# The order of the message sums on TensorE in a three-layer graph network kernel

## The chip, the cores and the metric

The kernel runs on one core of one Trainium2 chip. Time is device time in microseconds (us) of one execution; a comparison goes by the median of several runs. The profile is of one execution on the chip.

## What is computed

A graph network of three layers over 20,000 nodes with 512 features, and 5,000 edges sorted by their end node. Cut to what matters:

```
for Wl, bl, Wr, g, b in three layers:
    msg = h[src]
    agg = segment_sum(msg, dst) / max(count, 1)
    h   = residual + agg @ Wl.T + bl + h @ Wr.T
    h   = layer_norm(h, g, b)
    h   = prelu(h);  residual = h
out = layer_norm(x + h)
```

## The kernel before, in words

**Tiles and units.** Nodes are put into slots so that all nodes on which an edge ends lie in the first 40 tiles of 128 slots; the other tiles have no messages. Tiles are worked in pairs, called units. A layer has 20 *edge units* (two tiles with messages) and 59 *plain units*. The order of units is made by `order(lead)`: first `lead` plain units, then edge units with plain units between them. In the first two layers the lead is 20 units, and two plain units stand between an edge unit and the next. In the last layer the lead is 8 units, and of its 19 gaps between edge units 12 hold three plain units and 7 hold two. `Unit(no)` gives a unit's tiles, its layer and its buffers.

**TensorE** (`tensor_program`, the loop over T from L489 on) goes through the units; T is the unit in work, `ahead` is unit T+1. A step is:

- `turn(ahead)`: 8 transposes 128x128 of the next unit's rows (L402), into `ps_t`.
- If the next unit is an edge unit, `sum_messages(ahead, 0)` and `sum_messages(ahead, 1)`: 4 matmuls each (L414) that sum the gathered messages `msg[j]` by a 0/1-like matrix `same[j]` into `ps_s[j]`, one call for each tile j. Each waits for three things: the matrix (`e_same`, from VectorE), the gathered rows (`m_in[j]`, a DMA), and that the sums of the edge unit before were taken out of `ps_s[j]` (`e_carry`).
- `product_self(u, 0)`, `product_self(u, 1)`: the products of the unit in work with its own features, 12 matmuls of 512 columns for each tile (three for each of 4 chunks, since numbers are split into a high and a low part; L422, with `hT_hi`, `hT_lo`). They wait for `low` (the split, from VectorE) and `filled` (the bias rows, from ScalarE).
- For an edge unit in work, `product_mean(u, 0)` and `(u, 1)`: 12 such matmuls for each tile with the sums (L422, `sT_hi`, `sT_lo`).

All engines run their own written list in order, and meet by semaphores; TensorE passes its list strictly from top to bottom.

**GpSimd** (POOL) has, in step T: `root(T)` (L742; in the last layer also L746), then in the last layer `put_out` of unit T-5 (two indirect DMAs of output rows, L764), then in the first layer `gather_x`, then `gather_messages` of unit T+3 if that is an edge unit (two indirect DMAs, L731, one for each tile: `msg[0]`, then `msg[1]`). `gather_messages` waits until both sums of the edge unit before are done.

**SyncE** (SP) loads 512 KB of rows for a unit (`load_h`, L302), in the last layer also 512 KB for the residual (`load_residual`, L330), and for an edge unit 256 KB of row table (`load_rowtab`, L312), all in one list.

**VectorE and ScalarE** split the transposed rows (L535, L866), fill the bias (L575), take the squares of the products (L544), scale and shift (L877, L898), apply the prelu (L904), and for edge units make `same` (L915), carry the sums on (`carry`, L930) and split them (L584, L938).

The lines that order the work in a step of TensorE are:

Of the kernel before, what the change touches and what calls it, by code (L numbers as in the profile page):

```python
# [22 lines left out]
def reach(eng, sem, count):  # L23

    if count > 0:
        eng.wait_ge(sem, count)


def build_program(nc, x, wT, bl, g, b, a_prelu, ident_in, const_in, edge_cols_in, edge_last_in, edge_rows_in,
# [59 lines left out]
    with ExitStack() as ctx:  # L89
# [277 lines left out]
        def tensor_program(pe):  # L367
            def count_signs(i):

                pe.wait_ge(split_out, i + 1)  # L370
                begin, end = i == ET - SHARE, i == 2 * ET - SHARE - 1
                pe.matmul(signs_a, ones_short[:], tiles_above[i % HB], start=begin, stop=end)
                pe.matmul(signs_b, places_from[i % HB], tiles_above[i % HB], start=begin, stop=end).then_inc(counted, 1)
# [19 lines left out]
            def turn(u):  # L393
                if u.l == 0:
                    for j in range(u.n):
                        pe.wait_ge(x_in[u.r3][j], 16 * (u.no // 3 + 1))
                else:
                    pe.wait_ge(h_in[u.r3], 16 * (u.no // 3 + 1 - uses(u.r3, 3, UL)))
                reach(pe, low, u.no)
                for j in range(u.n):  # L400
                    for k in range(KC):
                        mm = pe.transpose(ps_t[:, j, k * P:(k + 1) * P], hin[u.r3][:, j, k * P:(k + 1) * P], ident[:])  # L402
                mm.then_inc(turned, 1)

            def sum_messages(u, j):
                if not u.edge:
                    return
                if u.eno == 0:
                    pe.wait_ge(table_done, 3)
                pe.wait_ge(e_same, 2 * u.eno + j + 1)  # L410
                pe.wait_ge(m_in[j], 16 * (u.eno + 1))
                reach(pe, e_carry, 2 * u.eno + j - 1)
                for k in range(KC):
                    mm = pe.matmul(ps_s[j][:, k * P:(k + 1) * P], msg[j][:, k * P:(k + 1) * P], same[j][:],  # L414
                                   start=True, stop=True)
                mm.then_inc(e_summed, 1)
# [9 lines left out]
            def product_self(u, j):  # L426
                if j >= u.n:
                    return
                if j == 0:
                    pe.wait_ge(low, u.no + 1)  # L430
                    if u.pos == 0:
                        pe.wait_ge(w_low, KC * (2 * u.l + 1))
                pe.wait_ge(filled, u.ahead + j + 1)
                mm = mm3(ps_z[u.r2][:, j, :], hT_hi[u.r2][:, j], hT_lo[u.r2][:, j], 2 * u.l, not u.edge)
                if not u.edge:
                    mm.then_inc(z_ready, 1)

            def product_mean(u, j):
                if not u.edge:
                    return  # L440
                if u.tiles[0] == 0 and j == 0:
                    pe.wait_ge(w_low, KC * (2 * u.l + 2))
                pe.wait_ge(e_low, 2 * u.eno + j + 1)
                mm3(ps_z[u.r2][:, j, :], sT_hi[j], sT_lo[j], 2 * u.l + 1, True).then_inc(z_ready, 1)

            def turn_table(parts):
                for j, (t0, t1) in enumerate(parts):
                    mm = pe.transpose(ps_s[0][0:t1 - t0, j * P:(j + 1) * P], table[:, t0:t1], ident[:])
                mm.then_inc(table_turned, 1)
# [31 lines left out]
            for T in range(UNITS):  # L481
                ahead, u = Unit(T + 1), Unit(T)
                if T == 0:
                    product_self(u, 0)

                    pe.wait_ge(row_step, 4)
                    pe.transpose(last_runs, run[:, P - 1:P], ident[0:ET, 0:ET]).then_inc(small, 1)
                if ahead.exists:
                    turn(ahead)  # L489
                if T == 0:  # L490
                    pe.wait_ge(row_step, 5)
                    pe.transpose(ahead_turned, runs_ahead[0:1, 0:ET], ident[0:1, 0:1]).then_inc(small, 1)
                for i in range(ET):
                    if T == COUNT_SLOT + 1 + i // COUNTS_A_SLOT:
                        if i == 0:
                            pe.wait_ge(table_done, 1)
                            pe.wait_ge(row_step, 6)
                        count_signs(ET - SHARE + i)
                if ahead.exists:
                    sum_messages(ahead, 0)  # L500
                if T > 0:
                    product_self(u, 0)
                if ahead.exists:
                    sum_messages(ahead, 1)
                product_self(u, 1)
                product_mean(u, 0)
                product_mean(u, 1)
                if T == TABLE_SLOT + 1:
                    pe.wait_ge(count_read, 2)
                    turn_table([(0, P), (P, NT)])  # L510
# [576 lines left out]
        with nc.Block() as block:  # L1087
            block.sync(sync_program)
            block.tensor(tensor_program)
            block.scalar(scalar_program)  # L1090
            block.gpsimd(gpsimd_program)
            block.vector(vector_program)
# [57 lines left out]
```

## Time and profile before

| | |
|---|---|
| median of 3 runs | 2011.26 us (2010.85 to 2011.39) |
| profiled execution, its own time | 2011.12 us |
| its span | 2009.3 us |
| TensorE matmul busy | 1974.9 us (98%) |
| VectorE busy | 1597.0 us (79%) |
| ScalarE busy | 1220.8 us (61%) |
| GpSimd busy | 924.1 us (46%) |
| matmuls of the sums (L414) | 960 records, 126.6 us busy |
| DMA, mean | 193 GB/s |

The profiled execution's own time is 1.8 us more than its span; what lies outside the span is taken as fixed. Times in the rows are counted from the start of the span. "Busy" of matmuls overlaps, as they are pipelined: what one costs is read from the distance between starts, not from its duration. One f32 matmul of L414 leaves two records.

The first layer lies at about 30 to 690 us, the second to about 1330 us, the last to 1980 us.

### The profile page before, as it was taken

What the parts mean: (1) busy time and instruction counts of PE and PEld (TensorE: products, weight loads), DVE (VectorE), ACT (ScalarE), POOL (GpSimd) and SP (SyncE); (2) the same over time, 40 slices, a digit from 0 to 9 for tenths busy, and PEclk for the clock granted to TensorE, in tenths of its full rate; (3) what the DMA queues carried; (4) which work ended last, traced back from release to release, by engine and by line L of the source; (5) the groups of instructions that cost most, each with busy time, mean ns of one, the idle gap of its engine ahead of it and who ended that gap; (6) DMA issues with size and microseconds to landing.
All of it is one profiled execution on the core that took longest, in us unless ns stands there. A gap on an engine that the chain in (4) does not pass through costs nothing. (4 is left out here: it accounts for less than half of the span.)

```text
span 2009.3 us, 30530 instructions
## 1 busy us (share of the span) xinstructions
PE 1974.9 (98%) x10207; PEld 1659.7 (83%) x10207; DVE 1597.0 (79%) x2598; ACT 1220.8 (61%) x2669; POOL 924.1 (46%) x887
## 2 busy tenths in 40 slices
PE   9999999999999999999999999999999999999994
PEld 7888888888888888888888888888888888888883
DVE  7778777777777677877777777769989998898985
ACT  6864545554444455544444444458878887787875
POOL 2666566556555411322333333215555455454555
PEclk9999999999999999999999999999999999999997
DMA  6667766766666555544444444456666666666652
GB/s 208 229 228 261 220 218 222 231 208 205 206 207 208 168 158 170 177 143 150 158 151 143 158 154 151 146 168 200 225 210 216 219 224 201 214 231 196 233 194 108
DMA packets 181075, 387.69 MB, mean 193 GB/s; under 512 B 20117, under 2 KB 20562, under 8 KB 180918
## 3 DMA queue, kind: packets, MB, share of 16 engines
q1 hardware_dynamic: 142358, 272.06, 40.6%
q0 software_dynamic: 38560, 113.67, 17.4%
q8 instruction: 82, 1.34, 0.3%
q14 instruction: 75, 0.61, 0.1%
HBM read 221.07 MB, written 164.79 MB: 192 GB/s over the span
## 5 line engine op out<-in xcount | busy, mean ns | idle before, releaser
L422 PE MATMUL ps_z<-w_hi,hT_hi 128*128 128x512 f32 x1884 | 763.0, 405 | 0.9 <-DVE hT_lo L866 0.6
L422 PE MATMUL ps_z<-w_hi,hT_lo 128*128 128x512 f32 x1884 | 738.6, 392 | 0.0
L422 PE MATMUL ps_z<-w_lo,hT_hi 128*128 128x512 f32 x1884 | 737.8, 392 | 0.0
L742 POOL TENSOR_TENSOR rstd<-veps,minus_half 128x2 f32<-128x2 f32 (+1 forms) x237 | 237.2, 1001 | 866.3 <-ACT veps L554 866.1
L866 DVE TENSOR_TENSOR hT_lo<-ps_t,hT_hi 128x1024 fp32r<-128x1024 f32 (+1 forms) x237 | 288.0, 1215 | 312.9 <-ACT hT_hi L535 309.5
L575 ACT COPY ps_z<-bias_rows 128x512 f32<-128x512 f32 x471 | 276.7, 588 | 344.6 <-DVE y L877 332.8
L544 ACT ACTIVATE junk<-ps_z 128x512 f32<-128x512 f32 x471 | 278.5, 592 | 307.1 <-PE ps_z L422 306.9
L422 PEld LDWEIGHTS ps_z<-w_hi,hT_lo 128*128 128x128 f32 x1884 | 353.5, 188 | 79.0
L422 PEld LDWEIGHTS ps_z<-w_hi,hT_hi 128*128 128x128 f32 x1884 | 354.5, 188 | 68.5 <-DVE hT_lo L866 1.0
L422 PEld LDWEIGHTS ps_z<-w_lo,hT_hi 128*128 128x128 f32 x1884 | 354.8, 188 | 67.0
L877 DVE SCALAR_TENSOR_TENSOR y<-ps_z,rstd,gain 128x512 f32<-128x512 f32 x471 | 330.1, 742 | 1.1 <-POOL rstd L742 1.0
L904 DVE SCALAR_TENSOR_TENSOR hout<-y,slope 128x1024 f32<-128x1024 f32 (+1 forms) x237 | 301.3, 1271 | 0.1
L898 DVE TENSOR_TENSOR y<-y,shift 128x1024 f32<-128x1024 f32 (+1 forms) x237 | 290.2, 1225 | 8.1
L402 PEld LDWEIGHTS ps_t<-ident,hin 128*128 128x128 f32 x1884 | 220.0, 140 | 31.8 <-issue 0.7
L402 PE MATMUL ps_t<-ident,hin 128*128 128x128 f32 x1884 | 244.4, 272 | 0.1
L535 ACT CAST hT_hi<-ps_t 128x1024 fp32r<-128x1024 f32 (+1 forms) x237 | 234.7, 990 | 6.3 <-PE ps_t L402 6.0
L764 POOL DMA_INDIRECT out<-o_sb,node_put x157 | 166.9, 1063 | 68.1 <-issue 50.7
L422 PE MATMUL ps_z<-w_hi,sT_lo 128*128 128x512 f32 x480 | 188.0, 392 | 0.0
L422 PE MATMUL ps_z<-w_hi,sT_hi 128*128 128x512 f32 x480 | 187.7, 391 | 0.0
L422 PE MATMUL ps_z<-w_lo,sT_hi 128*128 128x512 f32 x480 | 187.7, 391 | 0.0
L708 POOL DMA_INDIRECT hin<-in_x,node_get x157 | 157.2, 1001 | 63.4 <-issue 36.2
L611 ACT ACTIVATE o_sb<-o_sb,omove,rstd 128x512 f32<-128x512 f32 x157 | 119.6, 809 | 73.4 <-POOL omove L746 70.5
(147 smaller groups left out, 1927.6 us busy)
## 6 DMA issues: line engine op xcount, KB each, us to landing
h_scratch<-hout SPq DMA_DIRECT2D x156, 512.0 KB, 3.2
hin<-h_scratch SPq DMA_DIRECT2D x156, 512.0 KB, 4.3
x_by_slot<-hin SPq DMA_DIRECT2D x78, 512.0 KB, 3.2
o_sb<-x_by_slot SPq DMA_DIRECT2D x78, 512.0 KB, 4.6
rowtab<-edge_row_table SPq DMA_DIRECT2D x60, 256.0 KB, 4.7
stage<-in_WrT SPq DMA_DIRECT2D x3, 1024.0 KB, 8.8
stage<-in_WlT SPq DMA_DIRECT2D x3, 1024.0 KB, 7.5
hin<-in_x,node_get POOLq DMA_INDIRECT x157, 3.7
```

The source lines that it names most:

```text
L402: mm = pe.transpose(ps_t[:, j, k * P:(k + 1) * P], hin[u.r3][:, j, k * P:(k + 1) * P], ident[:])
L422: mm = pe.matmul(acc, a[:, k, :], ww[:, k, :], start=False, skip_group_check=True, stop=stop and k == KC - 1 and a is a_lo)
L535: nc.scalar.copy(hT_hi[u.r2][:, 0:u.n].rearrange("p j k n -> p (j k n)"), ps_t[:, 0:u.n, :].rearrange("p j d -> p (j d)")).then_inc(high, 1)
L544: nc.scalar.activation(junk[j][:], ps_z[u.r2][:, j, :], ACT.Square, accum_out=ssq[u.r2][:, j:j + 1]).then_inc(squared, 1)
L575: nc.scalar.copy(ps_z[u.r2][:, j, :], bias_rows[:, u.l, :]).then_inc(filled, 1)
L708: pool.indirect_dma_start(hin[u.r3][:, j, :], None, x, bass.IndirectOffsetOnAxis(node_get[:, t:t + 1], 0)).then_inc(x_in[u.r3][j], 16)
L742: nc.gpsimd.tensor_tensor(rstd[(T - 1) % 2][:, at], veps[(T - 1) % 2][:, at], minus_half[:, at], ALU.pow).then_inc(rstd_done, 1)
L764: pool.indirect_dma_start(out, bass.IndirectOffsetOnAxis(node_put[:, t:t + 1], 0), o_sb[u.ring][:, j, :], None, bounds_check=N - 1, oob_is ...
L866: nc.vector.tensor_tensor(hT_lo[u.r2][:, 0:u.n].rearrange("p j k n -> p (j k n)"), ps_t[:, 0:u.n, :].rearrange("p j d -> p (j d)"), hT_hi[ ...
L877: nc.vector.scalar_tensor_tensor(y[u.r2][:, j, :], ps_z[u.r2][:, j, :], rstd[u.r2][:, j:j + 1], gain[:, u.l, :], ALU.mult, ALU.mult).then_ ...
L898: nc.vector.tensor_tensor(y[u.r2][:, 0:u.n, :], y[u.r2][:, 0:u.n, :], moved, ALU.add).then_inc(shifted, 1)
L904: nc.vector.scalar_tensor_tensor(hout[u.r3][:, 0:u.n, :], y[u.r2][:, 0:u.n, :], slope[:, 0:1], y[u.r2][:, 0:u.n, :], ALU.mult, ALU.max).th ...
```

## The change

In a step whose next unit is an edge unit, TensorE now does the sums of both tiles one behind the other, and then the products of the unit in work. Before, the sum of tile 1 stood between the products of tile 0 and those of tile 1.

```diff
                 if ahead.exists:
                     sum_messages(ahead, 0)
+                    sum_messages(ahead, 1)
                 if T > 0:
                     product_self(u, 0)
-                if ahead.exists:
-                    sum_messages(ahead, 1)
                 product_self(u, 1)
                 product_mean(u, 0)
                 product_mean(u, 1)
```

No other engine's list changes. In TensorE's list this is the step ahead of the first edge unit, before (the rows of the twelve products that only repeat are left out):

```order
725 L414 MATMUL ps_s0<-same0,msg0 128x128 [waits m_in0,e_same,table_done]
726 L414 MATMUL ps_s0<-same0,msg0 128x128 x3
727 L422 MATMUL ps_z1<-w_hi0,hT_hi1 128x512 [waits filled,low]
...
738 L422 MATMUL ps_z1<-w_hi0,hT_lo1 128x512
739 L414 MATMUL ps_s1<-same1,msg1 128x128 [waits m_in1,e_same,table_done]
740 L414 MATMUL ps_s1<-same1,msg1 128x128 x3
741 L422 MATMUL ps_z1<-w_hi0,hT_hi1 128x512 [waits filled]
```

The sum of tile 1, with its wait for `m_in1`, stands behind the 12 products of tile 0. The same place in the changed kernel:

```order
725 L414 MATMUL ps_s0<-same0,msg0 128x128 [waits m_in0,e_same,table_done]
726 L414 MATMUL ps_s0<-same0,msg0 128x128 x3
727 L414 MATMUL ps_s1<-same1,msg1 128x128 [waits m_in1,e_same,table_done]
728 L414 MATMUL ps_s1<-same1,msg1 128x128 x3
729 L422 MATMUL ps_z1<-w_hi0,hT_hi1 128x512 [waits filled,low]
...
741 L422 MATMUL ps_z1<-w_hi0,hT_hi1 128x512 [waits filled]
```

The wait for `m_in1` now stands ahead of all 24 products of the step, and the number of instructions is the same. There are 60 such steps, 20 in each layer.

## Rows read from the trace of the kernel before

**Rows 1.** Last layer: stretch; PE, PEld, DVE, ACT, POOL busy; PEclk, DMA share, GB/s.

```profile
1400.00:1960.00 560.00, 560.00 (x2893) 474.66 (x2893) 510.78 (x928) 451.24 (x978) 300.66 (x306) 1.00 0.64 214
```

**Rows 2.** Timeline of PE (start, duration) around one edge step of the second layer.

```profile
1024.66 1.03 PE L402 MATMUL ps_t<-ident,hin 128*128 128x128 f32 x8
1025.53 1.06 PE L414 MATMUL ps_s<-same,msg 128*128 128x128 f32 x8
1026.35 0.48 PE L422 MATMUL ps_z<-w_hi,hT_hi 128*128 128x512 f32 x1
...
1032.79 1.03 PE L402 MATMUL ps_t<-ident,hin 128*128 128x128 f32 x8
1033.58 0.48 PE L422 MATMUL ps_z<-w_hi,hT_hi 128*128 128x512 f32 x1
...
1039.14 0.39 PE L422 MATMUL ps_z<-w_hi,sT_hi 128*128 128x512 f32 x1
```

**Rows 3.** Message gathers (L731) of the first layer, and its last sum's start on PE.

```profile
L731 POOL DMA_INDIRECT msg<-in_x,edge_cols x38: 952/1428/1950, 173.8 to 658.5; - x38
...
DMA to landing us min/median/max: 3.6/4.4/7.8
...
670.81 0.28 PE L414 MATMUL ps_s<-same,msg 128*128 128x128 f32 x1
```

**Rows 4.** The same for the second layer.

```profile
L731 POOL DMA_INDIRECT msg<-h_scratch,src_slot x38: 942/1018/1653, 824.9 to 1299.7; - x38
...
DMA to landing us min/median/max: 3.4/3.7/4.8
...
1314.61 0.28 PE L414 MATMUL ps_s<-same,msg 128*128 128x128 f32 x1
```

**Rows 5.** Last layer, first edge unit: gather of tile 1, sums on PE.

```profile
L731 POOL DMA_INDIRECT msg<-h_scratch,src_slot x1: 1910/1910/1910, 1377.8 to 1377.8; - x1
...
DMA to landing us min/median/max: 8.9/8.9/8.9
...
1382.57 1.06 PE L414 MATMUL ps_s<-same,msg 128*128 128x128 f32 x8
...
1386.82 1.13 PE L414 MATMUL ps_s<-same,msg 128*128 128x128 f32 x8
```

**Rows 6.** Last layer, third edge unit: gather of tile 1, first sum.

```profile
L731 POOL DMA_INDIRECT msg<-h_scratch,src_slot x1: 1907/1907/1907, 1435.9 to 1435.9; - x1
...
DMA to landing us min/median/max: 8.3/8.3/8.3
...
1442.18 0.28 PE L414 MATMUL ps_s<-same,msg 128*128 128x128 f32 x1
```

**Rows 7.** Last layer, 17th edge unit: gather of tile 1, first sum.

```profile
L731 POOL DMA_INDIRECT msg<-h_scratch,src_slot x1: 1911/1911/1911, 1860.9 to 1860.9; - x1
...
DMA to landing us min/median/max: 8.7/8.7/8.7
...
1867.22 1.06 PE L414 MATMUL ps_s<-same,msg 128*128 128x128 f32 x8
```

**Rows 8.** Timeline of SP at that place: loads issued.

```profile
1860.76 0.33 SPq L312 DMA_DIRECT2D rowtab<-edge_row_table  x1
1861.18 0.39 SPq L302 DMA_DIRECT2D hin<-h_scratch  x1
1861.66 0.42 SPq L330 DMA_DIRECT2D o_sb<-x_by_slot  x1
```

**Rows 9.** Busy time by stretch after PE's last matmul (columns of rows 1).

```profile
1980.30:1983.90 3.60, 0.00 (x0) 0.00 (x0) 3.50 (x7) 3.57 (x9) 2.71 (x5) 1.00 0.01 2
1984.00:1994.00 10.00, 0.00 (x0) 0.00 (x0) 5.10 (x12) 7.75 (x17) 7.80 (x11) 0.50 0.35 132
```

**Rows 10.** Timeline of PE at the start of the span.

```profile
2.22 2.07 PE L460 MATMUL ps_z<-nought,ones_full 128*128 128x512 f32 x4 [2.22 <-DVE ones_full L967]
...
10.16 0.24 PE L379 MATMUL ps_s<-sumT,twos_short 128*128 128x157 bf16 x1 [0.58 <-DVE sumT L833]
```

## Prediction

> **What bounds the kernel now.** I read the busy time by stretch first, then the timeline of TensorE (PE), then the message gathers and when they land. In the last layer PE is busy for all 560 us of the stretch, with VectorE (DVE) at 511 us and ScalarE (ACT) at 451 us [rows 1]; the granted clock is 1.00, the higher of the two levels. So PE sets the end. It is a list of work without holes, and a microsecond in which it waits in the middle moves everything behind it. The chain at the end, after PE's last matmul, starts from PE's last steps and moves along with them. What the change can do is therefore only two things: make PE's list itself shorter, or put a wait into it.
>
> **The list itself.** Nothing is added or removed; 60 calls of the sum of tile 1 move ahead of 12 products. A matmul's cost is the distance between starts. Before, such a step took from the first sum to the next transposes 1032.79 - 1025.53 = 7.26 us: sum, 12 products, sum, 12 products [rows 2]. After, it is sum, sum, 24 products. The last block of f32 work before products takes 1026.35 - 1025.53 = 0.82 us. One that has f32 work behind it has no such row for sums; the nearest is the transposes ahead of the sum, also 8 records, which take 1025.53 - 1024.66 = 0.87 us [rows 2]. The sum's own records stand slightly further apart than those of a transpose (0.82 us for a block of sums before products, 1033.58 - 1032.79 = 0.79 us for transposes), so I take 0.90 us. 24 products in one run take 1039.14 - 1033.58 = 5.56 us [rows 2]. Sum: 0.90 + 0.82 + 5.56 = 7.28 us, against 7.26. Bounds: if the first sum cost only 0.82, a step would take 7.20 and the kernel gain 60 x 0.06 = 3.6 us; at 7.28 it loses 1.2 us. The value nearest to all rows is no change, so this term is **0**, from -3.6 to +1.2 us.
>
> **The wait that moves.** The sum of tile 1 waits for three semaphores. `e_same` is no question: both matrices are made together, and the first sum, which needs its own of the pair, stands there already. `e_carry` asks for sums of the edge unit before, at least two steps back. The third is the gather of its 128 message rows. GpSimd issues it as the second of two, in the step three ahead of the edge unit, and it must land by the time PE has passed the first sum. Before, it had 3.6 us more, the first sum and 12 products. The queue behind the wait: all 24 products of the unit in work, the sum itself, and everything after, so a late gather costs its full lateness. It must land by (start of the first sum) + 0.90 us. Other engines have nothing to hide it with. I go by layer.
>
> First layer: gathers land after 7.8 us at the longest, and the last is issued at 658.5 for a first sum at 670.81, 12.3 us ahead [rows 3]. In time. Second layer: 4.8 us at the longest, and 14.9 us ahead (1299.7 for 1314.61) [rows 4]. In time with ten us to spare. So 40 of the 60 steps get no wait.
>
> Last layer: GpSimd has the output rows of an older unit to issue ahead of the gathers, and between many edge units stand three plain units instead of two, so that the gather goes out in a short plain step, not in the long step of an edge unit. There it leaves only 6.3 us ahead of the first sum and takes longer: 8.3 us at the third edge unit [rows 6], 8.7 us at the 17th [rows 7]. SyncE issues three loads, 1.25 MB, within 1.3 us of it [rows 8].
>
> - *First edge unit of the last layer.* Issued 1377.8, landed 8.9 us later at 1386.7; the second sum started at 1386.82, so it already waited for this landing by a little, and PE started it 0.1 us after the landing [rows 5]. After the change PE is ready at 1382.57 + 0.90 = 1383.47 and stands still for 3.35 us. Then it has still all 24 products to do where before it had 12, and 12 products are 5.56 / 2 = 2.78 us. Small holes that were there before (the step from 1382.57 to 1386.82 is 4.25 us where 3.63 is usual [rows 2]) are filled by this. Net **+2.7 us**.
> - *Third edge unit.* Landed 1435.9 + 8.3 = 1444.2, start of the sum 1444.3, ready at 1442.18 + 0.90 = 1443.1 [rows 6]: **1.2 us**.
> - *17th edge unit.* Landed 1869.6, start 1869.7, ready 1868.1 [rows 7]: **1.6 us**.
> - I worked out all 20 edge units of this layer in the same way. Between the third and the 17th, both counted, seven are late, by 0.2 to 1.6 us, 7.4 us together. All seven have three plain units ahead of them; five more of that kind are in time, the nearest by 0.35 us, and the seven edge units behind two plain ones have over 3 us to spare.
>
> Could the waits be won back? PE has no idle time to give and the others follow it; no.
>
> **Sum.** 2.7 + 7.4 + 0 = 10.1 us on the profiled execution's own 2011.12 us: 2021.2 us. The median of the runs lies 0.14 us above that execution. I say **2021 us**, 0.5% slower.
>
> A rule of the Trainium skill speaks to the 3.35 us wait. The row first: after PE's last matmul the granted clock stayed at 1.00 from 1980.3 to 1983.9 and was 0.50 after that [rows 9], so at least 3.6 us of idleness were borne at full clock; the longest wait forecast is a little shorter, so I add nothing for it. By the Trainium skill (TensorE: Matmul & The Clock Gate, "Why this matters for your kernels"), an idle stretch between bursts of matmuls of about this length puts the engine back to half clock; by that the sum would be higher, as the third rival below has it.
>
> **Rivals.**
>
> *The waits do not come, not slower.* The landing times are those of one pattern of DMA traffic. Once PE has stood still at the first edge unit, DVE, ACT and GpSimd could have caught up, so that later gathers go out earlier against PE's steps, or meet less traffic. It decides from 1.6 us: if the gathers of the last layer landed so much earlier against PE, only the first edge unit's 2.7 us would be left, 2013.8 us, within 0.2% of before (4.0 us, about what a measurement can tell from no change). For it: landings from the same distance differ by microseconds. Against it: the lead of 6.3 us is the same at the third and the 17th unit [rows 6, 7], 430 us apart, so the issue is tied to PE's own steps and moves with them. The Trainium skill (DMA: Bandwidth & Descriptors, "Issuing engines are not separate DMA queues") says that loads of SyncE and gathers of GpSimd run on the same engines and interleave; a shift of one against the other can thus go either way. 12%.
>
> *No wait and a shorter list, faster.* The 7.20 us step with no waits would give 2007.5 us. The first edge unit alone speaks against it, as its gather is issued from a point that nothing moves. 3%.
>
> *The clock falls.* If the 3.35 us wait brings PE to half clock, it stays there for a time. At the start of the span, 4 matmuls of 512 columns took 2.07 us [rows 10], about twice the 5.56 / 24 = 0.23 us each of rows 2, and the time until the fast ones from 10.16 on is under 8 us [rows 10]. So at most 4 us are lost: 2021.2 + 4 = 2025 us. 5%.
>
> *More gathers late.* The five that were in time fall behind as well, at about 1.1 us each like the others, or late ones become later: 2021.2 + 5.5 = 2026.7 us. 10%.
>
> **How the numbers follow.** The forecast gets 70%. Its own range is 2018 to 2024: a gather or two more or less, and the list term. Of 8 in 10, the range must reach into the other cases: the lower end at 2014, just above the case with the first wait alone, the upper at 2027. Slower by over 0.2% (over 2015.3 us): the forecast, the clock and the late gathers, 85%. Same: 12%. Faster: 3%.
>
> **What would show it.** In the changed profile the waits of PE must name `ps_s` L414 waiting for the DMA of `msg`, eight times, with the longest 3.3 us at the first edge unit of the last layer, and none in the first two layers. A step with both sums must take 7.2 to 7.3 us without a wait. PE's busy time in the last layer must fall short of the stretch by some 10 us, and the end of the second layer stay where it was. The forecast is wrong if the waits are short or absent in the last layer, if waits for `hT_lo` or `ps_z` come instead, or if edge steps of the first two layers change their length.

## Result, and the profile after

| | before | changed |
|---|---|---|
| median (6 runs each) | 2011.33 us | 2022.6 us |
| lowest to highest | 2010.85 to 2011.74 | 2020.82 to 2024.63 |
| profiled execution | 2011.12 us | 2020.82 us |
| its span | 2009.3 us | 2019.0 us |

The ratio is 1.0057 (95% interval 1.0046 to 1.0067): slower by 0.57%. The runs also lie further apart, 3.8 us instead of 0.9 us.

The profiled execution is the fastest of the six; its span grew by 9.7 us. First the waits of PE in the changed kernel (total, times, longest). Once the layers run, the list of before had only one wait of 0.6 us for `hT_lo` and one of 0.2 us for the bias rows:

```profile
PE ps_s L414 <- issue: 8.9, 8, 2.6
...
PE ps_z L422 <- DVE hT_lo L865: 0.6, 1, 0.6
```

The sums wait eight times. The view names no engine ("issue"), since the profile infers its releasers; that it is the message gather is shown by the landings below. These 8.9 us are idle time between the modelled ends of matmuls; by starts the waits are longer. Busy time by stretch shows the same, against [rows 1], which had PE busy for all 560 us. Here 6.5 us are missing; the longest wait lies ahead of this stretch:

```profile
1400.00:1960.00 560.00, 553.51 (x2844) 467.88 (x2843) 500.25 (x911) 443.09 (x957) 291.04 (x300) 1.00 0.64 210
```

The timeline of PE (start, duration) around the same step of the second layer as [rows 2]:

```profile
1023.90 1.04 PE L402 MATMUL ps_t<-ident,hin 128*128 128x128 f32 x8
1024.78 1.95 PE L414 MATMUL ps_s<-same,msg 128*128 128x128 f32 x16
1026.48 0.48 PE L422 MATMUL ps_z<-w_hi,hT_hi 128*128 128x512 f32 x1
...
1032.04 1.04 PE L402 MATMUL ps_t<-ident,hin 128*128 128x128 f32 x8
```

A step from the first sum to the next transposes takes 1032.04 - 1024.78 = 7.26 us, exactly as before: the two sums take 1.70 us, and 24 products in one run 5.56 us.

The gathers of tile 1 in the last layer (GpSimd's issue, and how long until it landed), at the first, third, 17th and 19th edge unit:

```profile
L730 POOL DMA_INDIRECT msg<-h_scratch,src_slot x1: 1910/1910/1910, 1376.9 to 1376.9; - x1
...
DMA to landing us min/median/max: 8.4/8.4/8.4
...
L730 POOL DMA_INDIRECT msg<-h_scratch,src_slot x1: 1907/1907/1907, 1437.1 to 1437.1; - x1
...
DMA to landing us min/median/max: 8.4/8.4/8.4
...
L730 POOL DMA_INDIRECT msg<-h_scratch,src_slot x1: 1906/1906/1906, 1868.3 to 1868.3; - x1
...
DMA to landing us min/median/max: 8.7/8.7/8.7
...
L730 POOL DMA_INDIRECT msg<-h_scratch,src_slot x1: 1908/1908/1908, 1928.8 to 1928.8; - x1
...
DMA to landing us min/median/max: 7.8/7.8/7.8
```

And the starts of the first and the second sum on PE at the first, third, 17th and 19th of them, and of the first sum at the last edge unit:

```profile
1381.67 0.28 PE L414 MATMUL ps_s<-same,msg 128*128 128x128 f32 x1
...
1385.35 0.35 PE L414 MATMUL ps_s<-same,msg 128*128 128x128 f32 x1 [2.62 <-issue]
...
1443.44 0.28 PE L414 MATMUL ps_s<-same,msg 128*128 128x128 f32 x1
...
1445.59 0.35 PE L414 MATMUL ps_s<-same,msg 128*128 128x128 f32 x1 [1.09 <-issue]
...
1874.65 0.28 PE L414 MATMUL ps_s<-same,msg 128*128 128x128 f32 x1
...
1877.05 0.35 PE L414 MATMUL ps_s<-same,msg 128*128 128x128 f32 x1 [1.35 <-issue]
...
1935.13 0.28 PE L414 MATMUL ps_s<-same,msg 128*128 128x128 f32 x1
...
1936.69 0.35 PE L414 MATMUL ps_s<-same,msg 128*128 128x128 f32 x1 [0.50 <-issue]
...
1968.47 0.28 PE L414 MATMUL ps_s<-same,msg 128*128 128x128 f32 x1
```

Without a wait the second sum starts 0.89 us behind the first. At the first edge unit it starts 3.68 us behind, 0.1 us after the landing at 1376.9 + 8.4 = 1385.3: a wait of 2.8 us. At the third the wait is 2.15 - 0.89 = 1.3 us, at the 17th 2.40 - 0.89 = 1.5 us, at the 19th 1.56 - 0.89 = 0.7 us. The other four (1.3, 0.8, 1.3 and 0.6 us) and a ninth of 0.3 us, read in the same way, bring the sum to 10.6 us. Against [rows 5 to 7] the landings are nearly the same: 8.4 us where it was 8.9, 8.4 (third unit) where it was 8.3, and 8.7 again.

In the kernel before, the first sum of the last edge unit started here:

```profile
1958.76 0.28 PE L414 MATMUL ps_s<-same,msg 128*128 128x128 f32 x1
```

From the first edge unit's first sum to this one it took 1958.76 - 1382.57 = 576.2 us [rows 5], and now takes 1968.47 - 1381.67 = 586.8 us: 10.6 us more, as much as the waits add up to.

In the first two layers no sum waits. Their gathers (compare [rows 3, 4]):

```profile
L730 POOL DMA_INDIRECT msg<-in_x,edge_cols x38: 954/1428/1947, 173.1 to 657.8; - x38
...
DMA to landing us min/median/max: 3.7/4.3/8.6
...
L730 POOL DMA_INDIRECT msg<-h_scratch,src_slot x38: 942/1018/1651, 824.3 to 1298.9; - x38
...
DMA to landing us min/median/max: 3.5/3.8/5.1
```

### The profile page after: what moved, and what is told of

Its sections match the earlier page's. It is cut to its first block and busy times, and to the rows that moved or that the text cites. A ratio compares the mean times of both kernels' runs of the same rounds, so it can differ in the third digit from the quotient of the medians.

```text
span 2019.0 us, 30530 instructions
## 1 busy us (share of the span) xinstructions
PE 1975.2 (98%) x10207; PEld 1659.3 (82%) x10207; DVE 1596.4 (79%) x2598; ACT 1221.0 (60%) x2669; POOL 924.1 (46%) x887
## 5 line engine op out<-in xcount | busy, mean ns | idle before, releaser
L610 ACT ACTIVATE o_sb<-o_sb,omove,rstd 128x512 f32<-128x512 f32 x157 | 119.6, 809 | 73.1 <-POOL omove L745 70.2
```

## Experiments

The theory: the loss is the wait for the gather of tile 1 in the last layer, and nothing else. The rivals: adjacent sums cost PE something in themselves; or VectorE and ScalarE, which get the products of tile 0 later, hand something over too late. "Before" is in each batch the kernel before on the same chip (medians 2010.85 to 2011.19 us). Each diff shows the lines that matter, against the changed kernel; where PE's order is that of before, the text says so.

**The sums together in the first two layers alone, and in the last layer alone.** The diff is of the first kernel; the second has `ahead.l == L - 1` in its first line. In the layers that are left out, PE's order is that of before.

```diff
+                early = ahead.exists and ahead.l < L - 1
                 if ahead.exists:
                     sum_messages(ahead, 0)
-                    sum_messages(ahead, 1)
+                if early:
+                    sum_messages(ahead, 1)
                 if T > 0:
                     product_self(u, 0)
+                if ahead.exists and not early:
+                    sum_messages(ahead, 1)
                 product_self(u, 1)
```

> The sums stand together in the first two layers only, 40 of 60 steps. Theory (the cost is waits for late message gathers, and these exist in the last layer alone): no wait of PE for messages, time within 1 us of before, 2010.3 to 2012.3 us. Rival (two sums one behind the other cost PE time in themselves, in any layer): two thirds of the loss, about 2018.5 us.

> The sums stand together in the last layer only, 20 of 60 steps. Theory: the whole loss, 2021 to 2023.5 us, with 8 to 10 waits of PE for messages of 0.2 to 3.3 us, together 10 to 11 us. Rival (a cost in every step): one third of the loss, about 2015 us.

Measured: first two layers 2010.78 us (ratio 0.9999, 0.999 to 1.0008); last layer 2022.89 us (ratio 1.0058, 1.0044 to 1.0072). A third of the steps carries the whole loss, two thirds carry none. The cost is not one of adjacency. The first kernel has one wait for messages of 0.3 us, against "no wait" in the expectation: in the last layer, at the first sum of the 13th edge unit, where its order is that of before. The gather of tile 0 can be a little late there in any order.

The waits of PE in the kernel with the last layer alone:

```profile
PE ps_s L414 <- issue: 9.4, 9, 2.8
```

This execution took 2023.5 us, 2.7 us more than the profiled one of the changed kernel, with nearly the same waits. The timeline of PE at the first edge unit of its last layer, and busy time by stretch there (columns of [rows 1], the granted clock third from the end), show where 1.4 us of it went; another 1.0 us had passed before this layer's first sum (1382.71 instead of 1381.67):

```profile
1382.71 1.06 PE L414 MATMUL ps_s<-same,msg 128*128 128x128 f32 x8
1386.61 2.04 PE L414 MATMUL ps_s<-same,msg 128*128 128x128 f32 x8 [2.85 <-issue]
1388.31 0.77 PE L422 MATMUL ps_z<-w_hi,hT_hi 128*128 128x512 f32 x1
1388.88 0.63 PE L422 MATMUL ps_z<-w_lo,hT_hi 128*128 128x512 f32 x1
1389.31 0.47 PE L422 MATMUL ps_z<-w_hi,hT_lo 128*128 128x512 f32 x1
```

```profile
1383.50:1386.50 3.00, 0.26 (x3) 0.07 (x1) 2.90 (x5) 3.00 (x9) 1.53 (x1) 0.93 1.05 386
1386.60:1389.30 2.70, 2.69 (x10) 2.52 (x11) 2.22 (x5) 2.13 (x5) 1.41 (x3) 0.50 0.47 188
1390.00:1393.00 3.00, 3.00 (x15) 2.46 (x14) 2.97 (x8) 3.00 (x8) 1.14 (x2) 1.00 0.77 194
```

The granted clock is 0.93, then 0.50, then 1.00 in the three stretches. It fell to the lower level (1.2 GHz) within the wait, which lasted 3.0 us by starts, and was back before 1390. The second sum took 1388.31 - 1386.61 = 1.70 us instead of 0.82, and the first two distances between products were 0.57 and 0.43 instead of 0.32 and 0.23. In the profiled execution of the changed kernel the wait of 2.8 us at the same place left the clock at 1.00.

**The gathers issued earlier.** PE keeps the changed order; GpSimd's list changes, in all layers.

```diff
-                old = Unit(T - 5)
+                old, soon = Unit(T - 5), Unit(T + 3)
+                if soon.exists:
+                    gather_messages(soon)
                 if old.exists:
                     put_out(old)
-                for stage_, ahead in ((gather_x, 3), (gather_messages, 3), (find_source, SRC_AHEAD)):
+                for stage_, ahead in ((gather_x, 3), (find_source, SRC_AHEAD)):
```

> The changed order on PE; GpSimd issues the two message gathers ahead of the two output stores of its step, about 2.6 us earlier. Theory: the second gather is issued about 9 us ahead of the first sum instead of 6.4, lands at least 2.6 us earlier, all waits for messages are gone: 2010.3 to 2012 us. Rival (what counts is the place of the sums on PE, through VectorE or ScalarE getting the products later): the time stays at 2021 to 2023 us.

A second kernel puts `gather_messages`, in the last layer, ahead of `root(T)` as well.

> The changed order on PE; in the last layer GpSimd issues the message gathers ahead of its root and its stores. Theory: no wait for messages, since a gather out by at least 2.6 us earlier is enough: 2010.3 to 2012 us, the same as with the gathers ahead of the stores alone. Rival (gathers that go out earlier meet other traffic, or the root that comes later delays VectorE): waits for messages or for hT_lo appear, over 2013 us.

Measured: 2010.21 us (ratio 0.9995, 0.9986 to 1.0004) and 2009.92 us (0.9994, 0.9984 to 1.0003). No wait for messages is left in either. The medians are a little below what was forecast; both are faster than before by 0.8 and 1.2 us, which is under 0.2%. In the first of them, the gathers of the last layer and the first sum of its last edge unit:

```profile
L730 POOL DMA_INDIRECT msg<-h_scratch,src_slot x36: 959/1000/1295, 1430.8 to 1948.3; - x36
```

```profile
1957.76 0.39 PE L414 MATMUL ps_s<-same,msg 128*128 128x128 f32 x2
```

The lead is 9.4 us, 3 us more than the 6.4 us of the kernel before. The order on PE that lost 11 us costs nothing with that. This is the strongest evidence for the theory: the products of tile 0 are as late for VectorE and ScalarE as in the changed kernel.

**The second sum half-way**, behind 6 of the 12 products of tile 0. `product_self` takes the chunks to work as one more argument; those lines are left out.

```diff
                 if ahead.exists:
                     sum_messages(ahead, 0)
-                    sum_messages(ahead, 1)
                 if T > 0:
-                    product_self(u, 0)
+                    product_self(u, 0, range(KC // 2))
+                if ahead.exists:
+                    sum_messages(ahead, 1)
+                if T > 0:
+                    product_self(u, 0, range(KC // 2, KC))
                 product_self(u, 1)
```

> The second sum stands behind the first 6 of the 12 products of tile 0, half-way between the two places, 1.4 us later than in the changed kernel. Theory: each wait is 1.4 us shorter. Of the measured ones (2.8, 1.3, 0.3, 1.3, 0.8, 1.3, 0.6, 1.5, 0.7 us) only the first keeps 1.4 us and one 0.1 us; with the holes that were there before already the time is 2011.8 to 2013.3 us. The more blocks of f32 work between products cost about nothing. Rival (the loss goes with the order, not with the distance): 2016 us or more.

Measured: 2012.64 us (ratio 1.0009, 1.0 to 1.0018), in the middle of what was expected. Its waits of PE:

```profile
PE ps_s L414 <- issue: 0.8, 1, 0.8
```

One wait is left, at the first edge unit, 1.3 us by starts. So the loss follows the distance between place and landing: 1.4 us more distance takes away most of it.

**Both sums together, but late**: between the products of tile 0 and tile 1.

```diff
-                if ahead.exists:
-                    sum_messages(ahead, 0)
-                    sum_messages(ahead, 1)
                 if T > 0:
                     product_self(u, 0)
+                if ahead.exists:
+                    sum_messages(ahead, 0)
+                    sum_messages(ahead, 1)
                 product_self(u, 1)
```

> Both sums stand together, but between the products of tile 0 and tile 1: adjacent, and not early. Theory: the messages of tile 1 must land by 3.6 us behind the step's transposes, as before, so no waits: 2010.3 to 2012 us. Rival (adjacent sums cost time): as the changed kernel, 2021 to 2023 us.

Measured: 2013.97 us (ratio 1.0013, 1.0004 to 1.0023). That is 2 us more than the top of the forecast: no wait for messages, but another cost that I had not counted. Waits of the other engines in the whole kernel:

```profile
ACT ps_z L574 <- DVE y L876: 436.0, 172, 5.6
...
DVE sumT L929 <- PE ps_s L414: 140.5, 49, 4.1
```

VectorE waits 140 us for sums where it waited 38 us before, since `carry` of the first sum stands in its list ahead of `take_low` and `normal`; ScalarE then waits 436 us for it instead of 333 us. Little of this reaches PE. PE's last matmul starts 1.9 us later than before (part of it is one wait of 1.0 us for the bias rows, in the step ahead of the last layer's first edge unit), and the end, which hangs on VectorE, comes another 0.9 us behind that. That `carry` is the cause is read from the list and not tested by itself. So the first sum is better early; the second has room, as the next kernel shows.

**The second sum behind all 24 products.**

```diff
                 if ahead.exists:
                     sum_messages(ahead, 0)
-                    sum_messages(ahead, 1)
                 if T > 0:
                     product_self(u, 0)
                 product_self(u, 1)
+                if ahead.exists:
+                    sum_messages(ahead, 1)
```

> The second sum stands behind all 24 products, 2.8 us later than in the kernel before. Theory: nothing waits for messages, the 0.3 us hole of the first edge unit of the last layer goes too, the sums' users on VectorE and ScalarE still have a step's products to work behind: 2010.3 to 2011.5 us. Rival (VectorE stands waiting for the later sum and hands over its splits too late): PE waits for sT_lo or hT_lo, over 2012 us.

Measured: 2010.69 us (ratio 0.9999, 0.9989 to 1.0008). As forecast, and no gain that can be measured.

**Less traffic beside the gathers.** The changed kernel with a quarter of each residual load.

```diff
-                sp.dma_start(o_sb[u.ring][:, 0:u.n, :], rows(xp_dram, u)).then_inc(xr_in[u.ring], 16)
+                cols = D if u.lap == 0 else P
+                sp.dma_start(o_sb[u.ring][:, 0:u.n, 0:cols], rows(xp_dram, u)[:, :, 0:cols]).then_inc(xr_in[u.ring], 16)
```

> The changed kernel, but the load of the residual in the last layer brings only 128 of the 512 columns, except for the first six units: three quarters of the residual rows are left out, 0.375 MB of the 1.25 MB that SyncE issues next to the second gather. Theory (the second gather lands late since it shares the DMA engines with these loads): at about 214 GB/s it lands up to 1.8 us earlier, most waits are gone, 2012 to 2016 us. Rival (the gather is slow in itself, behind GpSimd's own stores): landing after 8.3 us as before, 2021 to 2023 us.

This kernel leaves out three quarters of the residual rows of nearly all units of the last layer. Measured: 2012.25 us (ratio 1.0005, 0.9996 to 1.0015). By the starts on PE the second sum's wait at the first edge unit is 1.8 us, one of 0.7 us is left at the 13th, and the other seven are gone. (At the 13th the first sum waits a little too.) GpSimd issues its gathers at the same distance as before (6.35 us ahead at the last edge unit). So what made most of them late is the traffic of these loads. The trace of this run does not give the landing times themselves; that they come sooner is read from the sums that start without a wait.

**PE's order of before, with the early gathers.** The edit of GpSimd's list is that of the kernel with the gathers ahead of the root.

> PE in the order of the kernel before, and in the last layer the message gathers issued ahead of GpSimd's root. Theory: once the messages are there in time the place of the second sum is worth nothing, so the same as the changed order with early gathers, 2009.5 to 2010.5 us; against the kernel before only the 0.3 us hole at the first edge unit goes. Rival (two sums together do save time on PE once nothing waits): slower than the changed order with early gathers by over 0.5 us.

Measured: 2010.38 us (ratio 0.9997, 0.9988 to 1.0006); the changed order with the same gathers had 2009.92 us in another batch. Once the gathers are early, the two orders on PE are within 0.5 us of each other; each against before in its own batch, they are 0.7 us apart (-0.5 and -1.2 us). That two sums together save a few tenths of a us over the whole kernel is thus not excluded. The best of all kernels run is the one with the changed order and gathers ahead of the root, 0.06% faster than before, inside what a measurement can tell from no change.

**Another order of units in the last layer**, 20 plain units first and never three between edge units, with the changed order on PE and with that of before. The edit of the order is the same in both.

```diff
-    ORDERS = [order(LEAD)] * (L - 1) + [order(8)]
+    ORDERS = [order(LEAD)] * L
```

> The changed order on PE, and the last layer's units ordered as in the first two layers: 20 plain units first and then always two plain units between edge units, never three. Theory: no gather goes out in the step of a plain unit any more, each leads the first sum by 8.6 us or more and lands 3 us or more ahead of need; no waits for messages, the time within 1 us of the same units with PE's order of before (the run beside it). Rival (the last layer's traffic makes the gathers late wherever they stand): waits for messages of 0.5 us or more at several units, over 4 us slower than the run beside it.

> The same order of units in the last layer, PE's order of before: the partner of the run with 20 plain units first. Theory: both within 1 us of each other; against the kernel before within 3 us, since the amount of work is the same and only the end of the last layer has another mix of units. Rival: over 4 us faster than its partner.

Measured: 2021.51 us and 2020.42 us, 1.1 us apart. In the first, PE's waits:

```profile
PE ps_z L422 <- ACT ps_z L574: 4.9, 12, 0.6
...
PE ps_s L414 <- issue: 1.8, 1, 1.8
```

One wait for messages is left, at the first edge unit. I had forgotten it: that one has plain units ahead of it in any order, so its gather goes out in a plain step. At the other 19, leads are 6.9 us and more, and none waits. The eight waits behind the first edge unit all lie where three plain units stand together, and with two everywhere they are gone; but this layer also runs slower here, so the leads grew for that reason too (9.9 us and more at the third to 20th unit, where 8.6 us were expected). That both kernels are 10 us slower than before was not expected at all; it is told below.

**The first wait filled with work.** This kernel is the changed one, but does the first sum of the last layer's first edge unit four times.

```diff
+                times = 4 if u.eno == len(edge_units) * (L - 1) and j == 0 else 1
-                for k in range(KC):
+                for k in list(range(KC)) * times:
```

> The changed kernel, but at the first edge unit of the last layer PE does the first sum four times instead of once, 2.7 us of work in the place of most of its 2.8 to 3.0 us wait; all other waits stay. In one run with the same wait the granted clock had fallen to half after it, and the work of the next 3 us took 1.4 us longer. Theory (in part of the runs of the changed kernel that fall adds 1 to 2 us): here no run has it, the median is 2021.0 to 2021.8 us and the runs spread less, none above 2023 us. Rival (the spread comes from the landings alone): median 2022.4 to 2023 us and runs up to 2024.5 us, as the changed kernel.

Measured: 2021.3 us (2019.93 to 2022.96, 5 runs), against 2022.6 and 2022.89 us for the two kernels that have the whole wait. As the theory had it, the median is 1.3 us lower. But the ranges overlap, and these are medians of 5 or 6 runs; I take it as support, not as proof, that the clock falls in part of the changed kernel's runs.

The mean granted clock of each execution, measured with its time, says more. It is 0.993 or 0.994 in all 82 executions of the kernel before that ran beside the experiments. It is 0.992 in the slowest execution of the changed kernel (2024.63 us) and in two of the five with the last layer alone (2022.89 and 2024.6 us), and in no other. PE stands idle for 29.1 us behind its last matmul in the traces of both; half clock for all of that would give a mean of 1 - 0.5 x 29.1 / 2022.8 = 0.9928. So by this estimate the clock fell somewhere else as well in these three. With the profiled one (2023.5 us) the fall is there in at least 4 of the 11 executions that have the whole first wait, and in none of the 5 with the filled one does the mean show it.

## Why the prediction was right

**The list of PE costs nothing.** Forecast 7.28 us a step against 7.26; measured 7.26, with 1.70 us for two sums together where 1.72 was forecast. The kernel changed in the first two layers alone shows it as a time. One sentence of the prediction is off: it says that the gather had 3.6 us more before. Counted from the new place it was 3.63 - 0.90 = 2.7 us; the waits were worked out with the right distance.

**Forty steps without a wait.** Right: the waits listed for sums are all in the last layer, and the kernel changed in the first two layers alone loses nothing.

**The first edge unit of the last layer.** Forecast: a wait of 3.35 us, net +2.7. Measured in the profiled execution: 2.8 us. The gather landed 0.5 us sooner after its issue; from this first sum to the next edge unit's, the time grew by 29.15 - 27.00 = 2.15 us. In the execution of the last layer alone the wait was 3.0 us.

**The seven others.** Forecast 7.4 us. Measured at the same seven: 7.2 us. One that had been in time, the 19th edge unit, was late by 0.7 us, as the range allowed ("a gather or two more or less"). The landing times, which look like chance, repeat from one kernel to the other within 0.7 us at 18 of the 20 units, which fits that PE's step, GpSimd's issue and SyncE's loads keep the same distances; at the second one moved by 1.0 us, at the 19th by 2.3 us.

**The sum.** 10.1 us was forecast on the profiled execution, and its span grew by 9.7 us. That they come so near is in part luck. Between the last layer's first and last edge unit the change cost 10.6 us; but this execution was already ahead before that, by 0.7 us at the first sum of all (160.8 us, not 161.5) and by 0.9 us at the last layer's first. The first edge unit cost 0.5 us less than forecast, and the 19th 0.7 us that were not. The medians lie 11.3 us apart, 1.2 us more than the sum.

**The signs.** Eight waits were to be listed, and are, but the longest with 2.6 us, not 3.3, and by "issue", not by the DMA. PE's busy time was to fall short by some 10 us in the last layer: 6.5 us in the stretch shown, and the first wait ahead of it.

**The step that was too weak** is the one on the clock. I read from [rows 9] that 3.6 us of idleness are borne at full clock, added nothing, and gave a fall 5%. One profiled execution with a wait of 3.0 us had the fall; its price was 1.4 us, well within the 4 us at most that I had bounded it with. That the clock held for 3.6 us in one place was no bound for another: behind the last matmul it fell after 2.1 to 5.2 us in the 14 traces, in four of them within 2.8 us. By that count the case deserved nearer three in ten than 5%. It is also what the sum lacks: the forecast for the median had no term for it. By the rule of the Trainium skill (TensorE: Matmul & The Clock Gate, "Why this matters for your kernels"), which I had set aside, a wait of this length can bring half clock; the trace of the last layer alone agrees (3.0 us), while in the changed kernel's profiled execution the clock stayed at 1.00 in a wait of 2.8 us. It is probably part of why the median of the changed kernel is 1.8 us above its profiled execution; the filled wait and the mean clocks speak for it. Landings that differ from run to run add to it, and how much is each one's is open.

The rival by which the waits would not come is refuted by the eight waits. That with a shorter list fell with the 7.26 us. Of the five gathers that were in time, one became late, not five.

## What to carry to other kernels

A wait moved ahead of other work is priced by when its releaser lands, not by the waits that the profile lists: here the list of before showed next to none, while eight gathers landed too late for the new place, by up to 3.3 us. So for each moved wait, compare the landing with the new place, at every instance and in every stage, as the stage with the heaviest traffic decides. If an instruction is to move ahead on the engine that sets the time, move what it waits for first: the same order cost 11 us with late gathers and nothing with gathers issued 3 us sooner.

## What the runs showed of the hardware and the kernel that was not expected

- **The clock can fall in a wait of PE of 3.0 us**, and did not in one of 2.8 us, nor in 3.6 us after the last matmul of the kernel before. After the fall, sums and products took about twice as long until before 1390 us, 1.4 us lost in all. The idle time that it takes differs from one trace to the next. In the kernel with 20 plain units first and PE's order of before, PE's last matmul started at 1988.71 and ended 0.39 us later; the granted clock was already 0.50 some 2.1 us after that:

```profile
1988.71 0.39 PE L422 MATMUL ps_z<-w_hi,hT_lo 128*128 128x512 f32 x1
```

```profile
1989.10:1991.10 2.00, 0.00 (x0) 0.00 (x0) 1.97 (x3) 1.97 (x6) 1.79 (x4) 1.00 0.02 4
1991.20:1993.20 2.00, 0.00 (x0) 0.00 (x0) 1.90 (x2) 1.97 (x6) 1.82 (x2) 0.50 0.00 0
```

- **A single transfer's landing was mostly repeatable, and not always.** The gather of the 17th edge unit took 8.7 us before and in the changed kernel, 7 us later in the span. But that of the 19th took 5.5 and 7.8 us there, and in the kernel with the filled wait that of the 14th took 5.6 us instead of 7.8. Removing 0.375 MB of SyncE's loads for each unit took seven of nine waits away.
- **A long run of plain units in the last layer is slower than PE.** With 20 of them first, PE waits for the bias rows; busy time by stretch in the kernel with PE's order of before:

```profile
1385.00:1465.00 80.00, 75.29 (x362) 59.63 (x361) 73.07 (x117) 71.38 (x159) 42.96 (x46) 1.00 0.67 223
```

  PE is busy for 75.3 of 80 us, and a plain step takes 1423.72 - 1416.67 = 7.05 us instead of 6.33 us. The first edge unit comes 12 plain units later than in the kernel before, and its first sum 1467.88 - 1382.57 = 85.3 us later, where 12 x 6.33 = 76.0 us would do. These 9.3 us are nearly all of the 10 us by which those two kernels lose. A likely reason is that an edge unit's longer step lets VectorE (busy for 73.1 of the 80 us) and ScalarE (71.4) catch up; no kernel was run to test it. The starts of transposes and of that first sum:

```profile
1416.67 1.06 PE L402 MATMUL ps_t<-ident,hin 128*128 128x128 f32 x8
1418.11 0.47 PE L422 MATMUL ps_z<-w_hi,hT_hi 128*128 128x512 f32 x1 [0.37 <-ACT ps_z L575]
...
1423.72 1.06 PE L402 MATMUL ps_t<-ident,hin 128*128 128x128 f32 x8
...
1467.88 0.28 PE L414 MATMUL ps_s<-same,msg 128*128 128x128 f32 x1
```

  The 6.33 us, from the kernel before:

```profile
1735.85 1.03 PE L402 MATMUL ps_t<-ident,hin 128*128 128x128 f32 x8
...
1742.18 1.03 PE L402 MATMUL ps_t<-ident,hin 128*128 128x128 f32 x8
```

Open is how often the clock falls in the changed kernel's runs: a trace shows where it fell only for the profiled ones, and the mean granted clock gives no more than a lower count.
